# A graph kernel's gathers paced tile by tile: TensorE signals each tile, GpSimd waits for each tile

## The chip, the cores and the metric

The kernel runs on one core of a Trainium2 chip. The metric is the time on the device in microseconds (us), lower is better. The time of the kernel before is the median of three runs.

## The reference, cut to what matters

The inputs are 3125 nodes with 128 features each (`x`) and 53125 edges sorted by destination, each with a source, a destination, 128 attributes, a type (one of 32) and a weight. Two layers follow each other.

```
# layer 0
hsrc = x[src];  coef = w_comp[etype]                  # 8 coefficients for each edge
msg  = sum over b of (hsrc @ weight[b]) * coef[:, b]  ;  msg = msg * norm
x1   = layernorm(x + relu(segment_sum(msg, dst) + bias))
# layer 1
neigh = segment_sum(x1[src] + edge_attr, dst)
h     = relu(batchnorm(((1 + eps) * x1 + neigh) @ W1 + b1))
out   = layernorm(x1 + h @ W2 + b2)
```

## The kernel before, in words

**Tiles, units, couples, groups.** The edges are cut into T = 416 tiles of 128. Two tiles are a unit (208 units), two units a couple (104 couples), four units a group (52 groups), and edges of one unit go to a window of 20 neighbouring nodes.

**The ring of gathered rows.** For every tile GpSimd issues one indirect DMA (line 716), which fetches the 128 rows `x[src]` from DRAM into one of 32 places of `gathered`. The ring holds RU = 16 units. `gather_unit(u)` issues the two gathers of unit u. The first 16 units are gathered without waiting as soon as the source numbers are there. From unit 16 on, line 714 waits until `sums_mm` shows that the couple which used the same places is done: one signal of TensorE lets four gathers go.

**The preparation.** The coefficients of all edges are made in 26 quads (QUADS). For each quad TensorE spreads the types (line 936), VectorE compares them with the relation numbers (line 1283), TensorE multiplies with the table of coefficients (line 971, twelve products, the last of which signals `coef_mm`), and after each second quad VectorE multiplies with the weights (line 1288). The main loop starts after the last quad. GpSimd issues the first 32 gathers meanwhile.

**The main loop.** It is written out by hand over the 208 units. For each unit TensorE multiplies the gathered rows with one-hot columns scaled by the coefficients (line 999, one product of 160 or 120 columns for each tile; the trace shows two MATMUL records for each product in 32 bits), then the edge attributes with plain one-hot columns (line 1005). Only the last product of a couple signals, with `sums_mm`. VectorE waits for it and adds the couple's two windows to the sums (line 1509). SyncE waits for it before it loads the attributes of a later group. For each unit TensorE also counts edges between blocks of nodes (line 1020), which signals `counts_mm`, and ScalarE copies these counts (lines 800 to 804). When the sums of a chunk of 512 nodes are complete, the first layer of that chunk is computed between the units (line 1029 and others), and products of the second layer's neighbour sums are put in as well (line 1053). After the last unit the late chunks, the last blocks, the hidden layer and the output follow, without gathers of this ring.

GpSimd does nothing else in the main loop than to issue gathers. The order on each engine is the order in the code.

Of the kernel before, what the change touches and what calls it, by code (L numbers as in the profile page):

```python
# [21 lines left out]
UNIT = 2  # L22
# [12 lines left out]
def gnn_resnorm_kernel(nc, x, src, dst, edge_attr, etype, norm, weight, w_comp, bias0,  # L35
# [34 lines left out]
    QUADS = TQ // 4  # L70
# [14 lines left out]
    RU = RING * GU  # L85
# [87 lines left out]
    with ExitStack() as ctx:  # L173
# [3 lines left out]
        def sem(name):  # L177
            return ctx.enter_context(nc.semaphore(name))
# [7 lines left out]
        def weighted_tiles(s, i):  # L186
            lo = s * HALF * B * sum(WIDTHS) + i * HALF * B * WIDTHS[0]
            return weighted_flat[:, lo:lo + HALF * B * WIDTHS[i]].rearrange("p (t b n) -> p t b n", b=B, n=WIDTHS[i])
# [164 lines left out]
        def unit_psum(u):  # L353
            return psum[:, u // 2 % 3, u % 2 * (B + 1) * WIN:(u % 2 + 1) * (B + 1) * WIN].rearrange("p (b n) -> p b n", n=WIN)
# [43 lines left out]
        coef_mm = sem("coef_mm")  # L398
# [5 lines left out]
        select_ready = sem("select_ready")  # L404
        counts_mm = sem("counts_mm")
        sums_mm = sem("sums_mm")
        added = sem("added")
        keys_ready = sem("keys_ready")
        adj_zeroed = sem("adj_zeroed")
# [65 lines left out]
        def wait_alone(engine, semaphore, value):  # L475

            engine.wait_ge(semaphore, value)
            engine.sem_inc(passed, 1)

        def read_flag(engine, which):  # L480

            engine.wait_ge(flag_ready, 1)
            return nc.values_load(wide_flag[0:1, 0:1], engines=(which,), min_val=0, max_val=1,
                                  skip_runtime_bounds_check_because="a comparison's result")
# [205 lines left out]
        @block.gpsimd  # L690
        def _(pool):
            nc.gpsimd.memset(ident[:, :], 0.0).then_inc(const_ready, 1)
            nc.gpsimd.memset(comp_diag[:, :, :], 0.0).then_inc(comp_zeroed, 1)
            pool.wait_ge(const_ready, 1)
            nc.gpsimd.affine_select(out=ident[:, :], in_=ident[:, :], compare_op=ALU.not_equal, fill=1.0,
                                    base=0, pattern=[[-1, P]], channel_multiplier=1).then_inc(const_ready, 1)
            IMPRECISE = dict(allow_small_or_imprecise_dtypes=True)
            nc.gpsimd.iota(iota_win[:, :], [[1, WIN]], base=0, channel_multiplier=0, **IMPRECISE).then_inc(const_ready, 1)
            nc.gpsimd.iota(iota_wide[:, :], [[1, WIDE]], base=0, channel_multiplier=0, **IMPRECISE).then_inc(const_ready, 1)
            nc.gpsimd.iota(wide_starts[:, :], [[WIDE, WIDES]], base=0, channel_multiplier=0, **IMPRECISE).then_inc(const_ready, 1)  # L700
            nc.gpsimd.iota(iota_col[:, :], [[1, 1]], base=0, channel_multiplier=1, **IMPRECISE).then_inc(const_ready, 1)
            for q in range(4):
                pool.wait_ge(const_ready, 6 + q)
                nc.gpsimd.iota(relation_col[32 * q:32 * q + 32, :], [[1, 1]], base=0, channel_multiplier=1,
                               **IMPRECISE).then_inc(const_ready, 1)
            pool.wait_ge(const_ready, 10)
            nc.gpsimd.iota(iota_key[:, :], [[1, PITCH]], base=0, channel_multiplier=0, **IMPRECISE).then_inc(const_ready, 1)
            nc.gpsimd.memset(zero_col[:, :], 0.0).then_inc(const_ready, 1)
            nc.gpsimd.memset(ln_eps_col[:, :], LN_EPS).then_inc(const_ready, 1)

            def gather_unit(u):

                if u >= RU:
                    pool.wait_ge(sums_mm, (u - RU) // 2 + 1)
                for t in range(u * UNIT, (u + 1) * UNIT):
                    pool.indirect_dma_start(  # L716
                        gathered[:, t % (RING * GROUP), :], None, x[:, :],
                        bass.IndirectOffsetOnAxis(src_i[:, t:t + 1], 0)).then_inc(gather_in[u % RU], 16)


            pool.wait_ge(src_i_ready, 1)
            for u in range(RU):
                gather_unit(u)
            wide = read_flag(pool, ENGINE.Pool)
            with pool.If(wide < 1):
                for u in range(RU, U):
                    gather_unit(u)
            with pool.Else():
                for s in range(RU):
                    pool.wait_ge(gather_in[s], 16 * UNIT)  # L730
                for r, table in enumerate((x, x1_table)):
                    if r == 1:

                        pool.wait_ge(x1_out[0], 16 * (CHUNKS // 2 + 2))
                        pool.wait_ge(x1_out[1], 16 * (CHUNKS // 2 + 1))
                    with pool.Fori(0, T) as t:
                        wait_alone(pool, wide_slot[r], t + 1)
                        pool.indirect_dma_start(
                            gathered[:, 0, :], None, table[:, :],
                            bass.IndirectOffsetOnAxis(src_slots[:, 0:1], 0)).then_inc(wide_gather[r], 16)  # L740
# [179 lines left out]
        def _(pe):  # L920
# [32 lines left out]
            for k in range(2):  # L953
# [3 lines left out]
                             start=True, stop=True).then_inc(turned, 1)  # L957
# [27 lines left out]
            def narrow_sums():  # L985
# [3 lines left out]
                def sums_of_unit(u):  # L989
                    g, s, w = u // GU, u // GU % 2, u // 2  # L990
                    pe.wait_ge(gather_in[u % RU], (u // RU + 1) * 16 * UNIT)
                    if u % GU == 0:
                        pe.wait_ge(attrs_in[s], (g // 2 + (2 if g + 1 == GROUPS else 1)) * 16)
                        pe.wait_ge(select_ready, g + 1)
                    if u % 2 == 0 and w >= 3:
                        pe.wait_ge(added, 2 * (w - 2))
                    ps = unit_psum(u)
                    for i in range(UNIT):
                        nc.tensor.matmul(ps[:, 0:B, STARTS[i]:STARTS[i] + WIDTHS[i]],  # L999
                                         gathered[:, (u * UNIT + i) % (RING * GROUP), 0:F],  # L1000
                                         weighted_tiles(s, i)[:, u % GU, :, :],
                                         start=(i == 0), stop=(i == UNIT - 1))
                    for i in range(UNIT):
                        j = (u * UNIT + i) % GROUP
                        last = nc.tensor.matmul(ps[:, B, STARTS[i]:STARTS[i] + WIDTHS[i]], attrs[:, s * GROUP + j, :],  # L1005
                                                hot_tiles(s, i)[:, u % GU, :],
                                                start=(i == 0), stop=(i == UNIT - 1))
                    if u % 2:
                        last.then_inc(sums_mm, 1)
# [704 lines left out]
```

## Time and profile before

| | us |
|---|---|
| time, median of 3 runs (lowest, highest) | 781.75 (780.35, 783.78) |
| the profiled execution, its own time | 781.48 |
| its span, first to last instruction | 779.7 |
| TensorE busy (matmul), VectorE, ScalarE, GpSimd | 585.2, 493.7, 297.0, 418.9 |
| mean granted TensorE clock | 0.834 of full speed |

The span is 1.8 us shorter than the execution's own time. The busy times are of the engines side by side, so they say nothing of what the end waits for: that is read from the waits and from the order of the instructions in time. The profile gives the end of a TensorE product by a model, and a line with `[idle before <-releaser]` says how long the engine had stood idle and what ended that. "remote" stands for an update that the profile could not put to an instruction by its time, "issue" for idle time in which nothing was waited for that the profile shows.

### The profile page before, as it was taken

How to read it: one execution, taken by the hardware profiler on the slowest of the kernel's cores; microseconds unless marked ns; L12 is line 12 of the kernel's file. 1: busy time of each engine (PE TensorE's matmuls, PEld its weight loads, DVE VectorE, ACT ScalarE, POOL GpSimd, SP SyncE). 2: the span in 40 equal slices, each digit the busy share in tenths (PEclk: the TensorE clock that was granted, in tenths of full speed). 3: DMA queues.
4: the chain of work that ended last, by engine and by line, in shares of the span. 5: the costliest groups of instructions: out<-in, count | busy, mean ns of one | idle time of the engine just before them, and what ended most of it. 6: DMA issues, size and time to landing. Idle time of an engine off the chain costs nothing.

```text
span 779.7 us, 13302 instructions
## 1 busy us (share of the span) xinstructions
PE 585.2 (75%) x3971; PEld 480.7 (62%) x3971; DVE 493.7 (63%) x1866; ACT 297.0 (38%) x672; POOL 418.9 (54%) x434
## 2 busy tenths in 40 slices
PE   4137877777878686888678877797787876999994
PEld 2025766655667574776556766666676665878764
DVE  7039666667569676777764887767774344536456
ACT  9502444544455444445443544345340000000074
POOL 6730767667667665766765666666656666100000
PEclk9998657677875788757889788999889888999998
DMA  4400335455454654545744647566565562463002
GB/s 115 108 25 2 99 117 147 119 158 149 133 145 119 189 170 149 163 131 161 217 134 126 203 136 221 167 200 200 153 199 161 181 203 71 126 240 129 2 1 83
DMA packets 97035, 108.21 MB, mean 139 GB/s; under 512 B 10805, under 2 KB 81446, under 8 KB 96962
## 3 DMA queue, kind: packets, MB, share of 16 engines
q1 hardware_dynamic: 80898, 79.25, 32.6%
q0 software_dynamic: 13312, 27.29, 12.8%
q10 hardware_dynamic: 2752, 0.79, 0.4%
q8 instruction: 34, 0.56, 0.3%
q14 instruction: 39, 0.32, 0.1%
HBM read 81.73 MB, written 25.56 MB: 138 GB/s over the span
## 4 chain that ended last, share of the span: by engine, by line
DVE 34%; PE 34%; another core or an unknown queue 12%; issue 10%; DVEq 4%; ACT 3%; DMA 1%; ACTq 0%; SPq 0%
PE psum L1053 11%; DVE etype_hot L1388 7%; PE psum L999 6%; DVE etype_hot L1385 5%; PE psum L1029 5%; PE psum L1005 5%; DVE sums_flat L1509 5%; PE psum L1020 3%; DVE adj_flat L1479 3%; DVE weighted L1307 3%; DVE adj_flat L1283 2%; DVEq L1482 1%; ACT adj_flat L804 1%; DVE sums_flat L1463 1%
## 5 line engine op out<-in xcount | busy, mean ns | idle before, releaser
L716 POOL DMA_INDIRECT gathered_flat<-in_x_dram,src_i x416 | 416.6, 1001 | 247.3 <-issue 106.2
L999 PE MATMUL psum<-weighted,gathered_flat 128*128 128x160 f32 (+1 forms) x832 | 178.0, 342 | 23.4 <-issue 21.0
L999 PEld LDWEIGHTS psum<-weighted,gathered_flat 128*128 128x128 f32 x832 | 156.6, 238 | 42.1 <-issue 39.7
L1509 DVE TENSOR_TENSOR sums_flat<-psum,sums_flat 128x180 f32 x208 | 71.9, 346 | 168.8 <-remote 90.8
L1020 PE MATMUL psum<-etype_hot 128*128 128x300 f16 (+2 forms) x624 | 119.2, 313 | 48.4 <-issue 26.2
L778 ACT ACTIVATE adj_flat<-zero_col 128x450 f16<-128x450 f32 x208 | 108.4, 579 | 107.9 <-DMA adjacency<-adj_flat 66.6
L1005 PEld LDWEIGHTS psum<-hot,attrs 128*128 128x128 f32 x832 | 136.5, 231 | 9.5 <-issue 9.4
L1005 PE MATMUL psum<-hot,attrs 128*128 128x20 f32 (+1 forms) x832 | 131.0, 273 | 7.7 <-issue 7.7
L1388 DVE TENSOR_SCALAR etype_hot<-iota_key,key_t 128x300 f16<-128x300 f16 (+1 forms) x416 | 131.9, 318 | 0.0
L1020 PEld LDWEIGHTS psum<-etype_hot 128*128 128x128 f16 x624 | 69.7, 132 | 68.9 <-issue 43.0
L1385 DVE TENSOR_SCALAR etype_hot<-iota_key,gathered_flat 128x128 f16<-128x128 f16 x416 | 108.8, 262 | 0.1
L802 ACT ACTIVATE gathered_flat<-psum 128x25 f16<-128x25 f32 x182 | 35.0, 192 | 190.7 <-remote 92.5
L804 ACT ACTIVATE adj_flat<-psum 128x475 f32 x182 | 107.5, 591 | 0.2 <-issue 0.2
L1053 PE MATMUL psum<-sums_flat 128*128 128x264 f16 x570 | 77.0, 292 | 18.7 <-DVE sums_flat L1463 14.1
L1053 PEld LDWEIGHTS psum<-sums_flat 128*128 128x128 bf16 x570 | 57.8, 104 | 34.6 <-issue 23.4
L1307 DVE TENSOR_TENSOR weighted<-hot,coef 128x640 f32<-128x640 f32 x104 | 72.6, 739 | 3.3 <-DVE hot L1297 1.5
L1479 DVE TENSOR_TENSOR adj_flat<-gathered_flat,adj_flat 128x25 f16 x182 | 47.8, 265 | 27.8 <-DVE adj_flat L1479 11.7
L1053 PE MATMUL psum<-coef,sums_flat 128*128 128x264 f16 x330 | 52.4, 318 | 14.4 <-DVE sums_flat L1463 11.4
L1029 PE MATMUL psum<-sums_flat,gathered_flat 128*128 128x512 f32 (+1 forms) x112 | 53.7, 616 | 8.1 <-DVE sums_flat L1463 8.1
L1463 DVE TENSOR_TENSOR sums_flat<-psum,sums_flat 128x132 f32 x130 | 38.3, 295 | 22.4 <-DVE sums_flat L1463 6.5
L1053 PEld LDWEIGHTS psum<-coef,sums_flat 128*128 128x128 bf16 x330 | 36.0, 112 | 25.5 <-issue 16.6
L1029 PEld LDWEIGHTS psum<-sums_flat,gathered_flat 128*128 128x128 f32 x112 | 20.9, 213 | 24.5 <-issue 24.4
(144 smaller groups left out, 345.6 us busy)
## 6 DMA issues: line engine op xcount, KB each, us to landing
attrs<-in_edge_attr_dram SPq DMA_DIRECT2D x51, 512.0 KB
adjacency<-adj_flat SPq DMA_DIRECT2D x26, 900.0 KB
sums_flat<-adjacency SPq DMA_DIRECT2D x13, 576.0 KB
gathered_flat<-in_x_dram,src_i POOLq DMA_INDIRECT x416
coef<-adjacency SPq DMA_DIRECT2D x23, 288.0 KB
sums_flat<-adjacency SPq DMA_DIRECT2D x5, 648.0 KB, 8.8
sums_flat<-adjacency SPq DMA_DIRECT2D x9, 288.0 KB
out_dram<-gathered_flat SPq DMA_DIRECT2D x6, 256.0 KB
```

Source lines behind the costliest of these rows:

```text
L716: pool.indirect_dma_start(gathered[:, t % (RING * GROUP), :], None, x[:, :], bass.IndirectOffsetOnAxis(src_i[:, t:t + 1], 0)).then_inc(gat ...
L778: piece = nc.scalar.activation(adj_ring[:, s, j * size:(j + 1) * size], zero_col[:, 0:1].to_broadcast([P, size]), ACT.Copy)
L804: nc.scalar.activation(target[:, :, bass.ds(places[u % GU] + 1, WIN - 1)], counts[:, :, 1:WIN], ACT.Copy).then_inc(counts_copied, 1)
L999: nc.tensor.matmul(ps[:, 0:B, STARTS[i]:STARTS[i] + WIDTHS[i]], gathered[:, (u * UNIT + i) % (RING * GROUP), 0:F], weighted_tiles(s, i)[:, ...
L1005: last = nc.tensor.matmul(ps[:, B, STARTS[i]:STARTS[i] + WIDTHS[i]], attrs[:, s * GROUP + j, :], hot_tiles(s, i)[:, u % GU, :], start=(i = ...
L1020: last = nc.tensor.matmul(adj_counts(u)[:, :, lo:hi], low_hot[:, u % KEYRING, i, :], source[:, :, lo - STARTS[i]:hi - STARTS[i]], start=(i ...
L1029: product = nc.tensor.matmul(bank, w_base[:, b, :], sums[:, b, k * CHUNK:k * CHUNK + n], start=(b == 0), stop=(b == B - 1))
L1053: product = nc.tensor.matmul(psum[:, bank, 0:BLOCK * SPAN], x1_part(k, c)[:, i * F:(i + 1) * F], counts[:, :, 0:SPAN], start=(h == tiles[0 ...
L1307: last = nc.vector.tensor_tensor(weighted_tiles(s % 2, i), hot_tiles(s % 2, i).unsqueeze(2).to_broadcast([P, HALF, B, n]), coef[:, g * GRO ...
L1385: nc.vector.tensor_scalar(low_hot[:, u % KEYRING, i, :], iota_key[:, 0:P], low_t[:, t:t + 1], None, ALU.is_equal)
L1388: last = nc.vector.tensor_scalar(key_hot[:, u % KEYRING, i, 0:n], iota_key[:, 0:n], key_t[:, t:t + 1], None, ALU.is_equal)
L1509: nc.vector.tensor_tensor(window, unit_psum(u), window, ALU.add).then_inc(added, 1)
```

## The change

It has two parts. In the main loop, each tile's product with `x` (line 999) now signals a new semaphore `tiles_read`, 416 signals in all, and the gather of tile t waits for the signal of tile t - 32, which used the same place of the ring, where two units' gathers waited for the couple's `sums_mm`. `sums_mm` itself stays, for VectorE and SyncE. In the preparation, the gathers of units 8 to 15 no longer go at once: unit u waits until `coef_mm` has reached 26 * (u - 7) // 8, that is 3, 6, 9, 13, 16, 19, 22 and 26 quads.

```diff
@@ gather_unit
-                if u >= RU:
-                    pool.wait_ge(sums_mm, (u - RU) // 2 + 1)
                 for t in range(u * UNIT, (u + 1) * UNIT):
+                    if u >= RU:
+                        pool.wait_ge(tiles_read, t - RU * UNIT + 1)
                     pool.indirect_dma_start(
                         gathered[:, t % (RING * GROUP), :], None, x[:, :],
                         bass.IndirectOffsetOnAxis(src_i[:, t:t + 1], 0)).then_inc(gather_in[u % RU], 16)
@@
             for u in range(RU):
+                if u >= RU // 2:
+                    pool.wait_ge(coef_mm, QUADS * (u + 1 - RU // 2) // (RU // 2))
                 gather_unit(u)
@@ sums_of_unit
                         nc.tensor.matmul(ps[:, 0:B, STARTS[i]:STARTS[i] + WIDTHS[i]],
                                          gathered[:, (u * UNIT + i) % (RING * GROUP), 0:F],
                                          weighted_tiles(s, i)[:, u % GU, :, :],
-                                         start=(i == 0), stop=(i == UNIT - 1))
+                                         start=(i == 0), stop=(i == UNIT - 1)).then_inc(tiles_read, 1)
```

## Rows read from the trace of the kernel before

**Rows 1.** The profile's first part: busy time, share of the span, instructions

```profile
PE 585.2 (75%) x3971; PEld 480.7 (62%) x3971; DVE 493.7 (63%) x1866; ACT 297.0 (38%) x672; POOL 418.9 (54%) x434
```

**Rows 2.** Gathers alone by stretch: stretch, its length, POOL busy (count), clock, DMA

```profile
197.80:389.80 192.00, 126.67 (x126) 0.75 0.54 159
389.80:593.80 204.00, 129.07 (x130) 0.87 0.57 173
```

**Rows 3.** Waits of GpSimd in the main loop, 77.8 to 683: us, times, longest

```profile
POOL gathered_flat L716 <- issue: 96.7, 316, 0.7
POOL gathered_flat L716 <- remote: 73.7, 47, 2.3
POOL gathered_flat L716 <- PE psum L1005: 64.5, 21, 31.2
```

**Rows 4.** Groups by line in the main loop, 77.8 to 683: busy, mean ns, idle

```profile
L716 POOL DMA_INDIRECT gathered_flat<-in_x_dram,src_i x384 | 385.7, 1004 | 234.9 <-issue 96.7 <-remote 73.7 <-PE psum L1005 64.5
```

**Rows 5.** TensorE in order of time, 130 to 138: start, us, idle before

```profile
130.05 0.75 PE L1020 MATMUL psum<-etype_hot 128*128 128x300 f16 x3
...
131.59 0.60 PE L1005 MATMUL psum<-hot,attrs 128*128 128x20 f32 x4
132.04 0.48 PE L1020 MATMUL psum<-etype_hot 128*128 128x300 f16 x3
...
133.22 0.79 PE L1020 MATMUL psum<-etype_hot 128*128 128x300 f16 x3
134.47 0.39 PE L999 MATMUL psum<-weighted,gathered_flat 128*128 128x160 f32 x1 [0.46 <-issue]
135.19 0.39 PE L999 MATMUL psum<-weighted,gathered_flat 128*128 128x160 f32 x1 [0.33 <-issue]
...
137.34 0.50 PE L1005 MATMUL psum<-hot,attrs 128*128 128x20 f32 x3 [0.54 <-issue]
```

**Rows 6.** GpSimd, then VectorE, in order of time, same stretch

```profile
135.44 0.94 POOL L716 DMA_INDIRECT gathered_flat<-in_x_dram,src_i  x1 [0.30 <-issue]
137.72 0.94 POOL L716 DMA_INDIRECT gathered_flat<-in_x_dram,src_i  x1 [1.34 <-remote]
...
137.59 0.83 DVE L1509 TENSOR_TENSOR sums_flat<-psum,sums_flat 128x180 f32 x2 [2.70 <-remote]
```

**Rows 7.** The main loop's first gathers in order of time, all engines, 80 to 83

```profile
81.19 0.89 PE L1005 MATMUL psum<-hot,attrs 128*128 128x20 f32 x4
81.80 0.95 POOL L716 DMA_INDIRECT gathered_flat<-in_x_dram,src_i  x1 [0.30 <-issue]
...
82.22 0.82 DVE L1509 TENSOR_TENSOR sums_flat<-psum,sums_flat 128x180 f32 x2 [1.85 <-issue]
```

**Rows 8.** The preparation in order of time, 16 to 52: GpSimd, TensorE, VectorE

```profile
26.96 0.95 POOL L716 DMA_INDIRECT gathered_flat<-in_x_dram,src_i  x1 [0.30 <-issue]
...
45.72 0.95 POOL L716 DMA_INDIRECT gathered_flat<-in_x_dram,src_i  x1 [0.30 <-issue]
...
16.65 0.53 PE L971 MATMUL psum<-comp_parts,adj_flat 128*128 128x32 bf16 x12
...
21.11 0.53 PE L971 MATMUL psum<-comp_parts,adj_flat 128*128 128x32 bf16 x12
...
40.50 0.18 PE L971 MATMUL psum<-comp_parts,adj_flat 128*128 128x32 bf16 x1 [2.61 <-issue]
...
27.89 0.75 DVE L1283 TENSOR_SCALAR adj_flat<-psum,relation_col 128x512 bf16<-128x512 f32 x1 [7.25 <-remote]
51.01 0.42 DVE L1288 TENSOR_TENSOR coef<-psum,norm_t 128x256 f32<-128x256 f32 x1 [22.37 <-remote]
```

**Rows 9.** The preparation after its gathers: us, busy PE, PEld, DVE, ACT, POOL, clock, DMA

```profile
51.00:70.60 19.60, 15.07 (x284) 10.75 (x284) 19.08 (x36) 0.00 (x0) 0.00 (x0) 0.99 0.01 3
```

**Rows 10.** The first and last gather of the main loop, in order of time

```profile
77.83 1.16 POOL L716 DMA_INDIRECT gathered_flat<-in_x_dram,src_i  x1 [31.17 <-PE psum L1005]
...
665.86 1.40 POOL L716 DMA_INDIRECT gathered_flat<-in_x_dram,src_i  x1 [0.30 <-issue]
```

More of the change, by code:

```diff
@@ L406, in gnn_resnorm_kernel @@
         sums_mm = sem("sums_mm")
+        tiles_read = sem("tiles_read")
         added = sem("added")
```

## The prediction

> **What bounds the kernel now.** I began with the busy times [rows 1]. No engine is full: TensorE has 75%, GpSimd 54%. So the end hangs on waits, and I looked for an engine whose work and waits together fill the main loop. It is GpSimd. Its 384 gathers of the main loop are busy for 385.7 us and have 234.9 us of idle time before them [rows 4]; of that, 31.2 us is the one long wait ahead of the first of them [rows 3]. The rest is 203.7 us, and 385.7 + 203.7 = 589.4 us is the whole stretch from the first of these gathers at 77.8 to the end of the last at 667.3 [rows 10]. The idle time has two kinds: 316 short gaps of 0.31 us between gathers that follow each other (96.7 us), and 67 stops that wait for TensorE, 47 + 20, of 73.7 + 33.3 = 107 us, 1.60 us each [rows 3]. The rate is steady: 126 gathers in 192 us and 130 in 204 us [rows 2], 1.52 and 1.57 us for a gather, though the second stretch has more of the other work in it. A loop that keeps its pace like this is held by one circle: four gathers, then a wait for the signal of a couple.
>
> Next I asked whether TensorE is really late at those stops. It mostly isn't. The couple's last product (line 1005) starts its group at 131.59 and is through by 132.2 [rows 5]. VectorE waits for its signal and starts at 137.59, GpSimd at 137.72 [rows 6], over 5 us later. Both are named as released from "remote", because the update came when no product ended. So signals of TensorE are held up. They come free 1.0 us or so after the last gather in a row has ended (135.44 + 0.94 = 136.4), and several at once. Meanwhile TensorE itself slows down: four signals were pending (the groups of line 1020 that start at 130.05, 132.04 and 133.22, and the one of line 1005 at 131.59), and from then on its products start only every 0.72 us (134.47, 135.19), with "issue" as the reason [rows 5]. When the gathers have just begun after a long rest there is no such delay: the couple that ends at 82.1 releases VectorE at 82.22 although a gather runs from 81.80 [rows 7].
>
> The preparation shows it in large. TensorE's products of the second quad end at 17.2, and VectorE, which waits for them alone, starts at 51.01 after 22.4 us of idling; before that it had stood still for 7.2 us up to 27.89 [rows 8]. The last gather ends at 46.67 [rows 8], 4.3 us before the release. From there on 19.6 us without a gather do all the rest of the preparation, VectorE busy for 19.08 of them [rows 9]. I take this as the rule of this kernel: while gathers follow each other, TensorE's signals get through seldom, and they get through when GpSimd rests.
>
> **The change, part by part.**
>
> *The waits of the main loop.* A wait instruction costs GpSimd nothing that the rows show (it lies in the 0.31 us gaps), and behind it are only further gathers. Nobody waits for those soon: the ring is 16 units deep, and TensorE's waits name no gather. What changes is how many signals are needed and how much each one lets go. Now TensorE gives 104 `sums_mm` and 208 `counts_mm`, 312 signals, and one of them frees four gathers. With the change it gives 416 more, 728 in all, 2.33 times as many, and four gathers need four of them. TensorE's slow walk starts at four pending signals: before, these four are more than a couple of work, afterwards they are about one unit (two tiles, one count, half a sum), so a row of gathers stops after two or three where it now runs four or eight.
>
> The price of a stop is 1.60 us less the short gap of 0.31 us that it replaces, 1.29 us [rows 3]. Upper bound: as many signals get through at each stop as now, so stops grow with the signals, 67 * 2.33 = 156, 89 more, +115 us. Lower bound: the new signals slip through in the first gather after a stop, as at 82.22 [rows 7], and no stop is added, 0; below that is the rival of pacing. I take the middle, because both are seen in the rows: 44.5 more stops * 1.29 = +57 us.
>
> *The signals on the products themselves.* The 416 increments ride on products that are there anyway. The row for them is line 1005's last product, which signals and is followed by line 1020 0.45 us after its group starts, with no idle time [rows 5]: 0 us. That is the cost while signals flow; where they are held up it is counted in the stops. The Trainium skill (Advanced Engine Details and Errata, DMA Bandwidth Details) gives a semaphore increment on trn2 an overhead of about one cycle. By that alone the 416 would be free and the sum would be that of the preparation only; the delay of over 5 us in this trace is nothing that an increment of one cycle would show.
>
> *The preparation.* The first 16 gathers go as before, the last ends before 26.96 [rows 8]. Unit 8 needs three quads. The third ended at 21.6, and its signal gets through when the gathers rest, near 28, where one came through before [rows 8]. So unit 8's two gathers end near 30. With the same 4.3 us behind the last gather the chain would go on at about 33.5 in place of 51.0, a gain of 17.5 us at most. Then the pairs of units 9 to 15 lie between the quads, six of them ahead of the last quad. Each pair is 2.5 us of GpSimd, and its stop another 1.3: if nothing is hidden, 6 * 3.8 = 23 us come back (a loss of 5). If each holds the chain for 1.6 us, 9.5 come back. Nothing says which; I take a gain of 8 us, bounds 17.5 and -5. The last pair falls on the first units, whose rows are wanted 15 units later; it is hidden.
>
> *Everything behind the last gather*, and the loads that SyncE starts on `sums_mm`, keep their order: 0.
>
> Sum: 781.5 (the profiled execution's own time, 0.3 below the median) + 57 - 8 = 830 us.
>
> **The rivals.**
>
> 1. *Signals cost nothing in the loop, the preparation gains.* Stops stay 67 and only the 32 first gathers are spread. For it: TensorE's real work does not change, and at 82.22 a signal gets through at once. Against it: the slow walk at four pending signals. 781.5 - 15 = 766 us. This ends on the other side. It decides when the loop's added stops stay below about 10 (10 * 1.29 = 13 us). It is also what the skill's one cycle would give.
>
> 2. *Pacing helps the loop too.* Gathers are let go one by one, so rows of gathers are short while a signal is held up, TensorE stands less in its slow walk, and tile signals come before the couple's end, when GpSimd now idles. Half of the stops vanish: 33 * 1.29 = 43, and the preparation gives 18: 720 us. Speaking for it is that 20 of the 67 stops do end at a product of TensorE [rows 3]; against it that the other 47 end with held-up signals.
>
> 3. *Every pair of tiles ends in a stop.* 192 stops, 125 more, +161 us: about 934 us. It needs that no signal slips through at all, against rows 7.
>
> 4. *No change to tell.* A few added stops eat the preparation's gain: 781 us.
>
> A page of the skill (VectorE: DVE Perf Modes, the TRN2 errata) advises to space dense completion increments of several engines, because one engine's can block another's. No row here shows a deadlock of that kind; were it at work in the loop, it would push towards rival 3.
>
> **How the numbers follow.** A difference within 0.5% (3.9 us) is about what a measurement of this kernel cannot tell from no change. Forecast (790 to 880): 0.51. Rival 1 (756 to 777): 0.24. Rival 2: 0.10. Rival 3 and what lies above 880: 0.06. Rival 4 and small changes of either sign: 0.09. Faster is 0.24 + 0.10 = 0.34, same 0.09, slower 0.51 + 0.06 = 0.57. The range takes the forecast and rivals 1 and 4, 0.84 in all: 756 to 880. The forecast's own range is 790 (two bounds near their favourable ends) to 781.5 + 115 - 17.5 = 879, so 880.
>
> **What the profile after would show.** Right, if GpSimd's waits in the loop are more than 67 in number, above 90, still near 1.6 us each, many of them released by line 999 or "remote", and if the gathers come in rows of two to four. Then the first gather to the last takes 620 us or more. TensorE's idle time by "issue" ahead of line 999 would be larger too. In the preparation VectorE's wait of 22.4 us should be down to 5 or so and come again in small pieces between the quads, and the loop's first gather, now at 77.8 [rows 10], should start between 60 and 75. Wrong, if the waits stay at 67 or fewer: then held-up signals are not a matter of how many there are, and the time comes out under 780. The most likely fault is the size of the loop's term, since it rests on how many signals slip through, which the rows show only in single cases.

## The result, and the profile after

The changed kernel takes 755.54 us (median of 4 runs, 755.11 to 758.68) where the kernel before took 781.57 us (4 runs, 780.35 to 783.78) beside it. The ratio is 0.9656, with a 95% interval of 0.9627 to 0.9686: 26 us, or 3.4%, faster. The profiled execution took 755.78 us, with a span of 754.0 us. I had forecast 830 us.

The profile's first part, against [rows 1]:

```profile
PE 571.4 (76%) x3971; PEld 473.0 (63%) x3971; DVE 497.4 (66%) x1866; ACT 296.4 (39%) x672; POOL 411.8 (55%) x434
```

The number of instructions is the same. TensorE is busy for 13.8 us less and GpSimd for 7.1 us less, so their shares rise only because the span is shorter. The mean granted clock was 0.848 in this execution and 0.834 in the one of before, but the other three executions of the changed kernel had 0.814 to 0.823 and took 755.1 to 758.7 us, so the clock does not make the gain. GpSimd's waits over the whole span (us in total, times, longest), against [rows 3], and its gathers of the main loop alone, against [rows 4]:

```profile
POOL gathered_flat L717 <- issue: 97.1, 307, 2.4
POOL gathered_flat L717 <- PE psum L1002: 60.5, 58, 2.3
POOL gathered_flat L717 <- remote: 58.6, 42, 2.1
POOL gathered_flat L717 <- PE psum L974: 11.3, 8, 3.6
```

```profile
L717 POOL DMA_INDIRECT gathered_flat<-in_x_dram,src_i x384 | 379.1, 987 | 209.2 <-issue 90.1 <-PE psum L1002 60.5 <-remote 58.6
```

Without the one ahead of the loop's first gather (1.04 us, below), the stops on tile products and "remote" are 99, where there were 67. But they add up to 60.5 + 58.6 - 1.0 = 118.1 us, 1.19 us each, where 67 had added up to 107 us, 1.60 each. The short gaps between gathers fell from 96.7 to 90.1 us and the gathers themselves from 385.7 to 379.1 us. So 11.1 us more of stops met 13.2 us less of the rest, and the stretch from the first of these gathers to the end of the last has hardly changed: 379.1 + 90.1 + 118.1 = 587.3 us, against 589.4 us. The same by stretch (length, POOL busy and count, clock, DMA share, GB/s), against [rows 2], 1.51 and 1.57 us for a gather as before:

```profile
175.00:367.00 192.00, 124.78 (x127) 0.81 0.52 154
367.00:571.00 204.00, 127.16 (x130) 0.86 0.58 179
```

Most of the gain lies ahead of this stretch. The preparation in order of time (start, us, idle before): GpSimd, VectorE and TensorE, against [rows 8] and [rows 10]:

```profile
25.19 0.95 POOL L717 DMA_INDIRECT gathered_flat<-in_x_dram,src_i  x1 [0.31 <-issue]
29.75 0.95 POOL L717 DMA_INDIRECT gathered_flat<-in_x_dram,src_i  x1 [3.61 <-PE psum L974]
...
52.76 0.95 POOL L717 DMA_INDIRECT gathered_flat<-in_x_dram,src_i  x1 [1.12 <-PE psum L974]
...
55.99 1.24 POOL L717 DMA_INDIRECT gathered_flat<-in_x_dram,src_i  x1 [1.04 <-PE psum L1002]
...
641.83 1.41 POOL L717 DMA_INDIRECT gathered_flat<-in_x_dram,src_i  x1 [0.30 <-issue]
```

```profile
22.00 0.59 DVE L1320 COPY norm_t<-psum 128x416 f32<-128x416 f32 x1 [5.62 <-remote]
...
29.90 0.41 DVE L1291 TENSOR_TENSOR coef<-psum,norm_t 128x256 f32<-128x256 f32 x1
...
52.53 0.42 DVE L1291 TENSOR_TENSOR coef<-psum,norm_t 128x256 f32<-128x256 f32 x1 [1.24 <-PE psum L974]
```

```profile
54.85 1.29 PE L1002 MATMUL psum<-weighted,gathered_flat 128*128 128x160 f32 x4 [3.33 <-DVE weighted L1310]
```

TensorE's first product of the loop in the kernel before, and the last group of tile products, before and then after:

```profile
72.44 1.29 PE L999 MATMUL psum<-weighted,gathered_flat 128*128 128x160 f32 x4 [2.32 <-DVE weighted L1307]
691.98 0.73 PE L999 MATMUL psum<-weighted,gathered_flat 128*128 128x160 f32 x4
666.28 0.73 PE L1002 MATMUL psum<-weighted,gathered_flat 128*128 128x160 f32 x4
```

VectorE's wait of 22.37 us ahead of its first coefficients is gone. They start at 29.90 instead of 51.01, 21.1 us sooner. This is so although the late updates now fall on an earlier place too: nothing ahead of the first two quads was changed, yet VectorE's copy to `norm_t` starts at 22.00, after a wait of 5.62 us by "remote", where it started at 15.22 in the kernel before. There is one trace of each kernel, so how far such places shift from one execution to the next is not known; the times of the executions agree within 0.5%. The seven pairs of gathers that now lie between the quads stretch the chain of coefficients from 19.15 us (51.01 to 70.16) to 22.63 us (29.90 to 52.53), so 3.5 us come back. That leaves 17.6 us: TensorE's first product of the main loop starts at 54.85 instead of 72.44. The last group of tile products starts at 666.28 instead of 691.98, so TensorE's way through the loop takes 611.4 us instead of 619.5, 8.1 us less. (The stretch of gathers is no measure for it: its first gather now waits for one tile and not for a couple, and comes 1.14 us behind the first product instead of 5.39.) Behind that group nothing changes any more: 17.6 + 8.1 = 25.7 us is the whole difference between the two spans.

The chain of waits that ended last, by engine, says where the time is that is not work. First before, then after:

```profile
DVE 34%; PE 34%; another core or an unknown queue 12%; issue 10%; DVEq 4%; ACT 3%; DMA 1%; ACTq 0%; SPq 0%
```

```profile
PE 43%; DVE 31%; issue 11%; another core or an unknown queue 6%; DVEq 5%; ACT 2%; DMA 1%; SPq 0%; ACTq 0%
```

"another core or an unknown queue" is how a late update looks here. The pieces of the chain in the preparation, start and us, before and then after:

```profile
20.65 7.22 another core or an unknown queue
28.64 22.34 another core or an unknown queue
```

```profile
16.45 6.29 issue
23.97 3.71 issue
```

So the wait of 22.37 us lay on the chain that set the end, and 29.6 us of late updates there became 10.0 us in which TensorE stood by "issue". In the rest of the chain late updates fell from about 64 us (12.0% of 779.7 less 29.6) to 48 us (6.4% of 754.0), though TensorE's way through the loop is only 8.1 us shorter. GpSimd is in neither chain. That alone does not clear it: the chain cannot say what stands behind an update whose source the profile doesn't find.

### The profile page after: what moved, and what is told of

It is laid out like the page before. It is cut to its first block, busy times and chain, and to the rows that moved or that the text cites. A ratio compares the mean times of both kernels' runs of the same rounds, so it can differ in the third digit from the quotient of the medians.

```text
span 754.0 us, 13302 instructions
## 1 busy us (share of the span) xinstructions
PE 571.4 (76%) x3971; PEld 473.0 (63%) x3971; DVE 497.4 (66%) x1866; ACT 296.4 (39%) x672; POOL 411.8 (55%) x434
## 3 DMA queue, kind: packets, MB, share of 16 engines
q0 software_dynamic: 13312, 27.29, 13.2%
## 4 chain that ended last, share of the span: by engine, by line
PE 43%; DVE 31%; issue 11%; another core or an unknown queue 6%; DVEq 5%; ACT 2%; DMA 1%; SPq 0%; ACTq 0%
PE psum L1056 11%; PE psum L1002 8%; DVE etype_hot L1391 7%; PE psum L1008 7%; PE psum L1032 6%; DVE sums_flat L1512 5%; DVE etype_hot L1388 5%; PE psum L1023 5%; DVE adj_flat L1482 3%; DVE weighted L1310 3%; PE psum L939 2%; DVEq L1485 1%; DVE sums_flat L1466 1%; PE psum L1186 1%
## 5 line engine op out<-in xcount | busy, mean ns | idle before, releaser
L717 POOL DMA_INDIRECT gathered_flat<-in_x_dram,src_i x416 | 409.5, 984 | 230.4 <-issue 97.1
L1023 PE MATMUL psum<-etype_hot 128*128 128x300 f16 (+2 forms) x624 | 114.8, 305 | 80.8 <-issue 34.8
L1002 PE MATMUL psum<-weighted,gathered_flat 128*128 128x160 f32 (+1 forms) x832 | 171.0, 336 | 5.6 <-DVE weighted L1310 3.3
L1002 PEld LDWEIGHTS psum<-weighted,gathered_flat 128*128 128x128 f32 x832 | 152.6, 233 | 19.8 <-issue 17.0
L1008 PEld LDWEIGHTS psum<-hot,attrs 128*128 128x128 f32 x832 | 132.8, 226 | 6.9 <-issue 6.7
L1391 DVE TENSOR_SCALAR etype_hot<-iota_key,key_t 128x300 f16<-128x300 f16 (+1 forms) x416 | 134.7, 326 | 0.0
L1008 PE MATMUL psum<-hot,attrs 128*128 128x20 f32 (+1 forms) x832 | 127.5, 269 | 7.1 <-issue 7.0
L1023 PEld LDWEIGHTS psum<-etype_hot 128*128 128x128 f16 x624 | 67.6, 129 | 100.3 <-issue 60.6
L805 ACT ACTIVATE gathered_flat<-psum 128x25 f16<-128x25 f32 x182 | 34.8, 191 | 197.5 <-remote 106.3
L1388 DVE TENSOR_SCALAR etype_hot<-iota_key,gathered_flat 128x128 f16<-128x128 f16 x416 | 105.5, 254 | 0.1
L1056 PE MATMUL psum<-coef,sums_flat 128*128 128x264 f16 x330 | 52.5, 321 | 13.2 <-DVE sums_flat L1466 8.0
```

The source lines that it names most:

```text
L717: pool.indirect_dma_start(gathered[:, t % (RING * GROUP), :], None, x[:, :], bass.IndirectOffsetOnAxis(src_i[:, t:t + 1], 0)).then_inc(gat ...
L1023: last = nc.tensor.matmul(adj_counts(u)[:, :, lo:hi], low_hot[:, u % KEYRING, i, :], source[:, :, lo - STARTS[i]:hi - STARTS[i]], start=(i ...
L1056: product = nc.tensor.matmul(psum[:, bank, 0:BLOCK * SPAN], x1_part(k, c)[:, i * F:(i + 1) * F], counts[:, :, 0:SPAN], start=(h == tiles[0 ...
L1388: nc.vector.tensor_scalar(low_hot[:, u % KEYRING, i, :], iota_key[:, 0:P], low_t[:, t:t + 1], None, ALU.is_equal)
L1391: last = nc.vector.tensor_scalar(key_hot[:, u % KEYRING, i, 0:n], iota_key[:, 0:n], key_t[:, t:t + 1], None, ALU.is_equal)
```

## The experiments

All of them ran on four chips (numbers 3, 7, 10 and 14), which I take to be others than that of the result, and there the kernel before takes 667 to 668 us (medians of 667.15, 667.92, 667.91, 667.64, 667.43 and 668.2 us, of 7 to 29 runs), not 781. I come back to what differs. Each ratio below is to the kernel before on the same chip, with its 95% interval.

### The two parts of the change, alone and together

The preparation's waits alone, in the kernel before:

```diff
             for u in range(RU):
+                if u >= RU // 2:
+                    pool.wait_ge(coef_mm, QUADS * (u + 1 - RU // 2) // (RU // 2))
                 gather_unit(u)
```

> Only the second part of the change: the gathers of units 8 to 15 wait for quads, the loop's waits stay those of a couple. Theory P (the preparation gives nearly all of it): the last multiplication of coefficients ends near 53 us instead of 70.6, the loop's 67 stops of 1.60 us stay, and the time is 18 us under before, 761 to 765. Rival L (the loop's finer waits carry a good part, 10 us or more): 770 or more. Rival S (my prediction's stops: the loop part costs and the preparation gives more than the whole): under 755.

> The change's waits of the preparation alone, in the kernel before. Where the kernel before takes about 781 us, theory P (the gain is the preparation's: the loop's first product comes 17.6 us sooner, at 54.85 instead of 72.44 us): 761 to 766 us; rival L (most of the gain is the loop's): 775 us or more. Where the kernel before takes 667 us: no change, within 0.3%.

> The change's waits of the preparation alone, once more, for a chip on which the kernel before takes about 781 us. There, theory P (the preparation carries most of the gain): 761 to 766 us; rival L: 775 us or more. Where the kernel before takes 667 us: within 0.3% of it.

Measured: 668.07 us, ratio 0.9999 (0.9978 to 1.0019); 667.31 us, 0.9998 (0.9972 to 1.0024); 667.53 us, 0.999 (0.9961 to 1.0019). No change on three chips.

The loop's signals and waits alone:

```diff
-                if u >= RU:
-                    pool.wait_ge(sums_mm, (u - RU) // 2 + 1)
                 for t in range(u * UNIT, (u + 1) * UNIT):
+                    if u >= RU:
+                        pool.wait_ge(tiles_read, t - RU * UNIT + 1)
@@ sums_of_unit
-                                         start=(i == 0), stop=(i == UNIT - 1))
+                                         start=(i == 0), stop=(i == UNIT - 1)).then_inc(tiles_read, 1)
```

> Only the first part: a signal for each tile and a wait for each tile, the preparation as before. Theory P: 775 to 780, since in the changed kernel the stretch from the loop's first product to its last gather is 588.4 us against 594.8 before; GpSimd's stops rise to about 100 and their sum stays near 107 to 119 us. Rival L: 770 or less. Rival S: over 785.

> The change's signals and waits of the loop alone, in the kernel before. Where the kernel before takes about 781 us, theory P: 773 to 780 us (it gives the 6 to 8 us that the preparation does not); rival L: 765 us or less; rival S (added stops of GpSimd cost, as I had predicted): 790 us or more. Where the kernel before takes 667 us: no change, within 0.3%.

> The change's signals and waits of the loop alone, once more, for a chip on which the kernel before takes about 781 us. There, theory P: 773 to 780 us; rival L: 765 us or less; rival S (added stops cost): 790 us or more. Where the kernel before takes 667 us: within 0.3% of it.

Measured: 666.02 us, ratio 1.0002 (0.9978 to 1.0026); 666.31 us, 0.998 (0.9959 to 1.0002); 666.39 us, 0.999 (0.9956 to 1.0025).

The signals without the new waits, that is the last line of this diff alone:

> The 416 signals are given and nobody waits for them; all waits as before. If signals are free: 780 to 783, stops 67. If each further signal that is held up brings TensorE's slow walk earlier: 790 or more, with more idle time by issue ahead of line 999's products. The difference between this run and the run of the loop part alone is then what the finer waits give.

Measured: 668.06 us, ratio 1.0015 (0.9996 to 1.0034).

The whole change:

> The changed kernel unaltered, beside the kernel before, on whichever chip the run falls. Theory H (TensorE's signals arrive late while gathers run, and the change only has an effect where they do): where the kernel before takes about 781 us, 753 to 759 us (ratio 0.962 to 0.969); where the kernel before takes about 667 us, as in the first four runs, a ratio within 0.3% of 1. Rival G (the gain is one of the gathers themselves and holds everywhere): a ratio of 0.96 to 0.98 also where the kernel before takes 667 us.

Measured: 667.01 us, ratio 0.999 (0.996 to 1.002). Where figures were expected for a kernel before of 781 us, these runs say nothing on them. Theory H held for a kernel before of 667 us: the whole change brings nothing, so rival G, a gain that is to be had everywhere, fell. Which part brings how much where the kernel takes 781 us, no run has tested; that stands on the accounts of the two traces above.

What differs is in the profile of the run with the signals alone. VectorE's first and last coefficients there:

```profile
21.32 0.40 DVE L1289 TENSOR_TENSOR coef<-psum,norm_t 128x256 f32<-128x256 f32 x1
...
40.08 0.42 DVE L1289 TENSOR_TENSOR coef<-psum,norm_t 128x256 f32<-128x256 f32 x1 [0.23 <-PE psum L972]
```

Its 32 first gathers follow each other without a rest as in the kernel before, and are about as long (985 ns in the mean). Yet VectorE has its coefficients at 21.32 us, without the 22.37 us of waiting of [rows 8]. Late updates don't occur, and no wait of GpSimd is put down to "remote". GpSimd's waits in the run with the preparation alone (`f2_prep_alone`), and then in that of the whole change, both on chip 7:

```profile
POOL gathered_flat L716 <- issue: 118.0, 387, 0.3
POOL gathered_flat L716 <- PE psum L1007: 34.2, 26, 5.8
```

```profile
POOL gathered_flat L717 <- issue: 92.1, 301, 0.7
POOL gathered_flat L717 <- PE psum L1002: 62.3, 109, 6.7
```

The tile-wise waits raise the stops from 26 to 109 and their sum from 34.2 to 62.3 us, and the medians are 667.31 and 667.01 us. With the short gaps the idle time is 152.2 and 154.4 us: it was cut into more stops, and hardly grew. This is the first direct evidence against my price of a stop, on a chip where updates are not late.

### How far GpSimd is from the path

The changed kernel without the loop's 384 gathers (TensorE's products then read rows of other tiles):

```diff
-                for u in range(RU, U):
-                    gather_unit(u)
@@
-                    pe.wait_ge(gather_in[u % RU], (u // RU + 1) * 16 * UNIT)
+                    if u < RU:
+                        pe.wait_ge(gather_in[u % RU], 16 * UNIT)
```

> The changed kernel without its 384 gathers of the main loop: units from 16 on multiply with rows that an earlier gather brought, so the sums are not the reference's. It shows what the gathers cost the loop in all. If the loop is held by gathers and held-up signals, it runs far faster: I expect 560 to 680 us, and no signal of TensorE that is late. If TensorE's own work held it, it would stay within 3% of 755.

> The changed kernel without the 384 gathers of the loop; the products take rows of other tiles, so the output is not the reference's. Theory H (the gathers hold up TensorE's signals): 660 to 680 us on any chip, so where the kernel before takes 781 us the whole difference to 667 us goes away with the gathers. Rival C (the chip that takes 781 us is slower in its engines or DMAs, gathers or not): 740 us or more on such a chip.

Measured: 661.68 us, ratio 0.991 (0.988 to 0.994), and 657.88 us in a single run on another chip, without an interval. GpSimd is busy for 33.2 us, where it was 419.7 us in the run with the signals alone on the same chip, and the end comes 5.5 to 10 us sooner than in the kernel before. With prompt signals the gathers are almost wholly hidden. Whether taking them out would bring 781 us down to this, as theory H has it, could not be seen on these chips.

Then I moved the waits. The loop's gather of tile t waits for tile t - 16, or t - 24, in place of t - 32, or for the last tile of the group it replaces:

```diff
-                        pool.wait_ge(tiles_read, t - RU * UNIT + 1)
+                        pool.wait_ge(tiles_read, t - RU * UNIT // 2 + 1)
@@ or
+                        pool.wait_ge(tiles_read, t - 3 * RU * UNIT // 4 + 1)
@@ or
+                        pool.wait_ge(tiles_read, (t - RU * UNIT) // GROUP * GROUP + GROUP)
```

> The changed kernel, but the loop's gather of tile t waits for the product of tile t-16 in place of t-32, so that GpSimd may run only half as far ahead. Theory O (where TensorE's signals aren't held up, GpSimd is off the path that sets the end and its stops cost nothing): where the kernel before takes 667 us, within 0.5% of it (664 to 670 us), with over 120 waits of GpSimd on the product and the same sum of about 60 to 70 us. Rival S (a stop costs the path its own length, as in my prediction): each added stop adds up to 1.3 us, 690 us or more. Where the kernel before takes 781 us: theory H (gathers are spread out, so signals pass sooner) 740 to 756 us; S 770 us or more.

> The changed kernel, but the loop's gather of tile t waits for the product of tile t-24 in place of t-32. After the run with t-16 (688 us against 667.9, TensorE waiting 23 us for late rows), theory D (GpSimd's stops are free as long as the gathers keep so many tiles ahead of TensorE): where the kernel before takes 667 us, 664 to 672 us, with TensorE's wait for gathered rows under 5 us. Rival S (each stop costs): between the two, 676 to 680 us. Where the kernel before takes 781 us: theory H (earlier stops spread the gathers out, signals pass sooner) 745 to 755 us, S 765 us or more.

> The changed kernel, but the loop's gathers wait once per group: eight gathers are let go by the eighth product of the group they replace, so GpSimd issues eight without a gap. Theory D: where the kernel before takes 667 us, 664 to 672 us, with fewer than 50 waits on the product. Theory H, where the kernel before takes 781 us: longer runs of gathers hold TensorE's signals longer, 765 to 790 us; rival S (fewer stops are cheaper): 740 to 752 us.

Measured: t - 16: 687.99 us, ratio 1.0313 (1.0273 to 1.0353). t - 24: 676.58 us, 1.0143 (1.0106 to 1.0179). By group: 672.46 us, 1.0076 (1.0055 to 1.0097). Theory O missed at t - 16. The sum that I forecast for GpSimd's stops was also too low: 81.2 us. Theory D missed too: t - 24 cost 9 us, not under 5, and the waits by group were 99, not under 50. What grows is TensorE's wait for rows that have not landed, which is not there at all with t - 32. Its row with the waits by group, then at t - 24, then at t - 16 (there with GpSimd's stops ahead of it), all from the waits between 50 and 640 us:

```profile
PE psum L1002 <- DMA gathered_flat<-in_x_dram,src_i: 3.6, 2, 1.8
```

```profile
PE psum L1002 <- DMA gathered_flat<-in_x_dram,src_i: 6.7, 3, 5.1
```

```profile
POOL gathered_flat L717 <- PE psum L1002: 81.2, 118, 14.2
...
PE psum L1002 <- DMA gathered_flat<-in_x_dram,src_i: 11.7, 6, 5.2
```

3.6, 6.7 and 11.7 us of such waits stand beside 4.8, 8.9 and 20.1 us of time; in the last, 8 us more than the waits is not accounted for. The stops themselves don't set the time: by group, at t - 24 and in the whole change they are 99, 105 and 109 of 60.0, 63.5 and 62.3 us, with 4.8, 8.9 and no microseconds lost. What a stop costs depends on whether the rows behind it are already awaited. That S's figure for t - 16 (690 us or more) and for t - 24 (676 to 680) came close is no support for it for this reason.

One more in the preparation: waits from unit 4 on.

```diff
-                if u >= RU // 2:
-                    pool.wait_ge(coef_mm, QUADS * (u + 1 - RU // 2) // (RU // 2))
+                if u >= RU // 4:
+                    pool.wait_ge(coef_mm, QUADS * (u + 1 - RU // 4) // (3 * RU // 4))
```

> The changed kernel, but in the preparation the gathers wait for coefficient products from unit 4 on instead of unit 8. Theory O, where the kernel before takes 667 us: no change, 664 to 670 us. Where the kernel before takes 781 us, theory P (in the preparation every run of gathers without a gap holds up the signals behind it): 745 to 755 us, as the first wait of VectorE for an update (5.6 us before 22.00) shrinks; rival: 755 to 760 us, since TensorE's coefficient products are not late by then.

Measured: 666.9 us, ratio 0.9987 (0.9959 to 1.0016). No change, as expected for a chip with prompt signals; its other half stays open.

### Late signals put in by hand

Since no chip of the experiments delayed signals, I made the delays of the two traces with waits. In the kernel before, VectorE's first coefficients wait until the rows of the 16 first units have landed. In the second kernel they wait for the first 8 units, with the change's waits of the preparation added:

```diff
             def coefficients(c):
                 dve.wait_ge(coef_mm, 2 * c + 2)
+                if c == 0:
+                    dve.wait_ge(gather_in[RU - 1], 16 * UNIT)
@@ the second kernel, with the preparation's waits of the change
+                    dve.wait_ge(gather_in[RU // 2 - 1], 16 * UNIT)
```

> The kernel before, with VectorE's first block of coefficients made to wait until the rows of all 16 units of the preparation have landed: this puts by hand, where signals are prompt, the delay that the trace of the kernel before shows at that place (first coefficients at 51.01 us, where on the chip with prompt signals they come at 21.32 and the last at 40.08). Theory E (a delay in the preparation reaches the end whole): last coefficients at about 71 to 73 us, so 31 to 33 us later, and 697 to 702 us. Rival F (the loop catches up, for it is not bound by the same chain): under 690 us.

> The same with the change's waits of the preparation, and the first coefficients waiting for the rows of the first 8 units only, which is where the changed kernel's first stop of GpSimd lies. Theory E: last coefficients at 47 to 50 us, 674 to 678 us, so 20 to 26 us under the other of the pair (the trace of the changed kernel has 52.53 against 70.16, 17.6 us). Rival F: the two within 10 us of each other.

Measured: 691.86 us, ratio 1.0363 (1.0291 to 1.0436), and 672.46 us, 1.0061 (1.0035 to 1.0088). The first coefficients and the loop's first product in order of time, first kernel and then second:

```profile
47.77 0.42 DVE L1290 TENSOR_TENSOR coef<-psum,norm_t 128x256 f32<-128x256 f32 x1 [26.69 <-DMA gathered_flat<-in_x_dram,src_i]
...
68.82 1.28 PE L999 MATMUL psum<-weighted,gathered_flat 128*128 128x160 f32 x4 [2.31 <-DVE weighted L1309]
```

```profile
28.38 0.42 DVE L1292 TENSOR_TENSOR coef<-psum,norm_t 128x256 f32<-128x256 f32 x1 [7.01 <-DMA gathered_flat<-in_x_dram,src_i]
...
49.48 1.28 PE L1001 MATMUL psum<-weighted,gathered_flat 128*128 128x160 f32 x4 [2.36 <-DVE weighted L1311]
```

The loop starts 19.3 us apart and the medians lie 19.4 us apart. The first kernel's time is known to about 5 us only (its interval), and the two profiled executions lie 16.8 us apart, so between these two a delay in the preparation reaches the end whole or nearly so. Against the kernel with prompt signals, whose loop starts at 42.36, the loop starts 26.5 and 7.1 us later and the time is 23.7 and 4.3 us longer, so some 3 us of each delay seem to be swallowed, which is within the interval of the first and just beyond that of the second. The times came out some 5 and 2 us under what I had set for E, since those 3 us are lost and the last coefficients of the first kernel came at 66.55 us and not at 71 to 73. The difference of the pair is just under the 20 to 26 us that I had set for theory E, and F, within 10 us, fell. This makes it likely that the preparation's 17.6 us on the chip of the result reached the end; there itself no run has shown it, only the chain of waits.

For the loop, VectorE's add of each couple waits until the last two of the four gathers that the couple lets go have landed, first in the kernel before, then with the change's signals and waits of the loop:

```diff
                     dve.wait_ge(sums_mm, w + 1)
+                    if 2 * w + 1 + RU < U:
+                        dve.wait_ge(gather_in[(2 * w + 1) % RU], ((2 * w + 1) // RU + 2) * 16 * UNIT)
```

> The kernel before, with VectorE's add of each couple's sums made to wait until the four gathers that this couple lets go have landed: late signals in the loop put by hand. Theory K (late reads of TensorE's results set the loop's pace on the slow chip, through the adds and the PSUM they free): well over the 667 us of the kernel before, 700 to 790 us. Rival: GpSimd's gathers are fast enough behind the products, 667 to 680 us.

> The same with the change's signals and waits of the loop: gathers let go tile by tile begin up to 2.8 us sooner than by couple, so the adds too. Theory K: 5 to 30 us less than the other of the pair. Rival S (the added stops of GpSimd cost): the same time as the other or more.

Measured: 946.79 us, ratio 1.4147 (1.4092 to 1.4201), and 859.69 us, 1.2878 (1.2808 to 1.2948). The waits and the chain by engine, first by couple and then by tile:

```profile
POOL gathered_flat L716 <- PE psum L1005: 306.6, 66, 11.3
DVE sums_flat L1511 <- DMA gathered_flat<-in_x_dram,src_i: 298.6, 64, 13.4
```

```profile
PE 36%; DMA 18%; DVE 17%; POOL 15%; issue 11%; ACT 2%; DVEq 1%; POOLq 0%; SPq 0%; ACTq 0%
```

```profile
POOL gathered_flat L717 <- PE psum L1000: 239.6, 151, 8.6
DVE sums_flat L1512 <- DMA gathered_flat<-in_x_dram,src_i: 223.4, 56, 11.7
```

```profile
PE 40%; DMA 21%; DVE 18%; issue 8%; POOL 6%; ACT 2%; DVEq 2%; ACTq 0%; POOLq 0%; SPq 0%
```

The delay put in is cruder than the real one and costs far more (947 us against 781, and far outside the 700 to 790 us that I had expected), so these two give a direction and no size. The direction is plain. Where a circle really closes over the gathers, their share shows in the chain (POOL 15%), and the tile-wise waits take 87 us off. They do it with more than twice as many stops, 151 against 66. I had expected 5 to 30 us.

## Why the prediction was wrong

**The step that failed** is the term of the loop, "44.5 more stops * 1.29 = +57 us". It takes every added stop to lengthen the loop by its own length, because "a loop that keeps its pace like this is held by one circle: four gathers, then a wait for the signal of a couple". Measured where the change was timed: 32 more stops, and with the short gaps the idle time between the gathers grew from 203.7 to 208.2 us. That is 4.5 us, 0.14 us for each added stop and not 1.29. The gathers themselves took 6.6 us less, so their stretch is 2.1 us shorter, and TensorE's way through the loop is 8.1 us shorter, not 57 longer. That busy and waiting time of GpSimd add up to the length of the loop (589.4 us) is no sign that GpSimd sets it. An engine that waits for another's tiles fills the loop with stops whatever their number. The chain of waits of before, which the prediction does not use, had no share of GpSimd in it. On the chips with prompt signals the step fell by runs as well: the sum of the stops went from 34.2 to 62.3 us at no cost, and without the gathers the kernel took only 1 to 1.5% less. Whether GpSimd has a part in the pace of the loop on the chip of the result in another way, through the late updates, is open.

**The number of stops** was forecast well: over 90, many of them released by the product or by "remote". With it went a size that didn't hold, 1.6 us each, and it was 1.19. The finer wait cut nearly the same idle time into more pieces. So the sign I had named for being right (over 90 waits) appeared, and the time that I had tied to it did not: the first gather to the last takes 587.3 us and not 620 or more. Nor did the sign for being wrong (67 waits or fewer) appear, though the time is under 780 us.

**The signals on the products** were rightly put at 0. In the run with the signals alone they cost between nothing and 2.3 us (ratio up to 1.0034), for 416 of them, on a chip where updates are not late. The Trainium skill (TensorE: Matmul & The Clock Gate, The cost: per-tile semaphore tail) gives 26.3 ns for each completion increment of packed products. An estimate by that is 416 * 26.3 ns = 10.9 us if all of it lay on the path, which the run rules out.

**The preparation** had the right direction and the wrong size. I put 17.5 us for the start of the coefficients less 9.5 for the pairs of gathers between them, 8 us. Measured were 21.1 less 3.5, 17.6 us, just beyond my upper bound of 17.5. Two sizes were off. I counted the 4.3 us of the first release from the end of unit 8's gathers, and so had 33.5; the coefficients start at 29.90, 3.8 us behind the last gather ahead of the stop (26.14) and together with unit 8's first (29.75). And each pair held the chain for 0.5 us instead of 1.6. That such a gain reaches the end whole I had taken for granted; the pair with delays put in supports it, within the 5 us said there. The rule behind the term, that updates get through when GpSimd rests, holds only roughly: one reached VectorE at 22.00 us in the changed kernel, while a gather of the first run was under way (21.44 to 22.39).

**The slow walk of TensorE** from four pending signals on, from which I had the number of stops, did not grow. The profile's groups had 23.4 us of idle time ahead of the tile products before, 21.0 of it by "issue"; now it is 5.6 us, with 3.3 of it by VectorE. Ahead of the counts' products "issue" rose from 26.2 to 34.8 us:

```profile
L1023 PE MATMUL psum<-etype_hot 128*128 128x300 f16 (+2 forms) x624 | 114.8, 305 | 80.8 <-issue 34.8
L1002 PE MATMUL psum<-weighted,gathered_flat 128*128 128x160 f32 (+1 forms) x832 | 171.0, 336 | 5.6 <-DVE weighted L1310 3.3
```

By "issue" the two together fell from 47.2 us to at most 37.1, where I had said that this idle time would grow ahead of the tile products. The rest of what grew ahead of the counts' products is waiting for VectorE and ScalarE.

**The rivals.** Rival 1 comes nearest, 766 us, but its condition was fewer than 10 added stops, and there were 32. What it had right is that most of the gain is that of the preparation. Rival 2's mechanism, earlier tile signals, shows in the pair with delayed adds (-87 us); in the result all that the loop gives is 8.1 us and not 43, and no run says how much of it is due to that mechanism. None of the rivals has the sum as it came, the preparation's 17.6 us and 8.1 us of the loop. I gave the two a third of the chance together.

**What stays open** is why TensorE's updates are late where the kernel takes 781 us and not where it takes 667, whether the gathers have a part in it, and, since of all kernels only the two compared ran there, what each part of the change is worth there by itself. The account of 17.6 and 8.1 us is read from two traces.

## What to carry over

An engine whose busy time and waits add up to the loop is not yet the one that sets it: look whether it is in the chain of waits, and ask who would be late if it stopped longer. Price a finer wait by how late its release comes to the one who needs the data, not by the number of stops. And a few stops in a long run of background gathers beside a chain of short steps are worth trying, as long as the rows aren't awaited yet: here they cost nothing where signals are prompt, and where they are late the kernel with them, and with the finer waits of the loop, was 26 us faster.

## What the hardware showed beside this

The same kernel took 781.57 us where the two kernels were compared and 667.15 to 668.2 us on the four chips of the experiments. I speak of another chip; that it is the chip, and not something else about its setting, is an assumption. A gather takes the same on both, 1004 ns in the loop of the one and 1005 ns on another (the run with the signals alone). TensorE is busy for 585.2 us at a granted clock of 0.834 on the one and for 532.8 us at 0.872 on the other, so it does its work more slowly there too; how much of that is cause and how much follows from the waiting, between products that come in pieces, isn't settled. One part can be placed: the loop's first product starts at 72.44 against 42.36 us, 30 us that hang on updates which VectorE saw up to 22 us late. On the other chips equally long runs of gathers delay nothing. So the gathers alone are not the cause, and my rule that signals get through when GpSimd rests describes, and only roughly, the traces of the result. No run here says what the other condition is.
